# Fused look-ups in a product-key search: 128 narrow instructions a tile in place of 12 wide ones

## What is computed

```python
scores, idx = top_k(sim, 16)              # sim: (2, ..., 8 heads, 64 keys)
index = idx[0][:, None] + 64 * idx[1][None, :]      # 16 x 16 candidates
score = scores[0][:, None] + scores[1][None, :]
final_scores, pk_idx = top_k(score, 16)
final_indices = take_along_axis(index, pk_idx)      # the look-up
k = einsum(softmax(final_scores), keys_table[final_indices + head * 4096])
v = einsum(softmax(final_scores), values_table[...])
```

## Time and profile before

| | |
|---|---|
| median of 3 runs | 8583.4 us (8580.13 to 8584.05) |
| profiled execution, its own time | 8587.36 us |
| its span, first to last instruction | 8585.5 us |
| DVE busy | 4933.7 us, 57% of the span, 16123 instructions |
| PE busy | 6138.6 us, 71% |
| POOL busy | 5943.7 us, 69%, of which 6144 gathers |
| ACT busy | 3293.3 us, 38% |

### The profile page before, as it was taken

How to read it: one execution, slowest core, us unless ns; L and a number is a source line. 1 busy time by engine, 2 the same in 40 slices (tenths; PEclk the granted TensorE clock), 3 DMA queues, 4 the chain that set the end, 5 groups by cost and what they waited for, 6 DMA issues and landing times.

```text
span 8585.5 us, 111803 instructions
## 1 busy us (share of the span) xinstructions
PE 6138.6 (71%) x30064; PEld 4636.8 (54%) x30064; DVE 4933.7 (57%) x16123; ACT 3293.3 (38%) x9885; POOL 5943.7 (69%) x6159
## 2 busy tenths in 40 slices
PE   6869979787887879687887879787886875233222
PEld 5648656666565647666565656656465652122112
DVE  1246484947566574847566574857667473646522
ACT  1213334444443444434443444444443443333232
POOL 0007667777777777777777777777777777777775
PEclk7765666666766666566766666566766665555555
DMA  1102222222222222222222222222222222121111
GB/s 30 17 4 65 52 53 58 59 61 60 63 60 58 60 59 61 60 61 60 62 59 58 59 60 61 60 61 60 60 60 58 61 59 53 52 53 52 52 53 41
DMA packets 660626, 471.64 MB, mean 55 GB/s; under 512 B 560624, under 2 KB 561008, under 8 KB 659632
## 3 DMA queue, kind: packets, MB, share of 16 engines
q0 software_dynamic: 196608, 403.05, 17.8%
q1 hardware_dynamic: 463344, 60.87, 4.5%
HBM read 461.32 MB, written 2.10 MB: 54 GB/s over the span
## 4 chain that ended last, share of the span: by engine, by line
POOL 59%; issue 20%; PE 14%; DVE 4%; SPq 1%; DVEq 1%; ACT 1%; DMA 1%; POOLq 0%; ACTq 0%
POOL GATH L700 59%; PE MM L477 3%; PE MM L492 1%; DVE KV L923 1%; PE PB L1320 1%; PE PB L1308 1%; PE PB L1256 1%; PE PB L1287 1%; PE MM L429 1%; PE MM L513 1%; PE MM L516 1%; PE PB L1328 1%; PE MM L452 1%; PE TP L486 1%; SPq L371 0%
## 5 line engine op out<-in xcount | busy, mean ns | idle before, releaser
L700 POOL DMA_INDIRECT GATH<-in_table,IDX x6144 | 5937.5, 966 | 2590.9 <-issue 2505.0
L916 ACT ACTIVATE GATH<-GATH,WT 128x128 f32<-128x128 f32 x6144 | 1884.1, 390 | 1966.9 <-DMA GATH<-in_table,IDX 1966.1
L923 DVE TENSOR_REDUCE KV<-GATH 128x128 f32<-128x2048 f32 x384 | 1392.0, 3625 | 1165.3 <-ACT GATH L916 1157.7
L477 PE MATMUL MM<-SPEC,SW 128*128 128x8 f32 (+1 forms) x8800 | 1150.8, 288 | 103.0 <-DMA SW<-in_sw 68.9
L477 PEld LDWEIGHTS MM<-SPEC,SW 128*128 128x128 f32 (+1 forms) x8800 | 1143.0, 248 | 141.1 <-issue 138.3
L586 DVE COPY TURN<-TP 80x512 f32<-80x512 f32 (+1 forms) x512 | 345.1, 684 | 451.5 <-PE TP L509 275.0
L1423 PE MATMUL PB<-AREA 128*64 128x64 f32 (+1 forms) x2304 | 320.3, 300 | 392.1 <-ACT AREA L1198 391.9
L1423 PEld LDWEIGHTS PB<-AREA 128*64 128x64 f32 (+1 forms) x2304 | 257.7, 194 | 474.4 <-issue 426.0
L429 PE MATMUL MM<-F,TURN 128*128 128x80 f32 x2048 | 371.1, 341 | 197.4 <-DVE TURN L586 192.4
L429 PEld LDWEIGHTS MM<-F,TURN 128*128 128x128 f32 x2048 | 341.9, 252 | 249.4 <-issue 186.6
L545 ACT ACTIVATE U<-MM 128x320 f32<-128x320 f32 (+1 forms) x416 | 218.8, 526 | 636.7 <-PE MM L429 388.1
(11 more groups left out here) (223 smaller groups left out, 10065.5 us busy)
## 6 DMA issues: line engine op xcount, KB each, us to landing
GATH<-in_table,IDX POOLq DMA_INDIRECT x6144
SW<-in_sw SPq DMA_DIRECT2D x1280, 40.0 KB
CONV<-in_cwb SPq DMA_DIRECT2D x128, 4.0 KB
CONV<-in_cwb SPq DMA_DIRECT2D x128, 0.1 KB
U<-in_xT SPq DMA_DIRECT2D x16, 96.0 KB
out<-OUTB SPq DMA_DIRECT2D x16, 96.0 KB, 1.9
W1E<-in_w SPq DMA_DIRECT2D x1, 512.0 KB
W2E<-in_w SPq DMA_DIRECT2D x1, 512.0 KB
```

Source lines behind the costliest of these rows:

```text
L477: m = e.matmul(pv[r, :, k, :], SW[r, half, k % HM, w:w + WID * beside], Sv[r, :, c * MODES + k, :], start=True, stop=True)
L700: e.indirect_dma_start(GATH[:, r, k, :], None, table, bass.IndirectOffsetOnAxis(IDX[:, u // H, u % H, k:k + 1], 0)).then_inc(gath[r], 16)
L916: m = e.activation(GATH[:, r, k, :], GATH[:, r, k, :], ACT.Copy, scale=WT[:, u // H, u % H, k:k + 1])
L923: e.tensor_reduce(KV[:, u // H, :, u % H, :], GATH[:, u % RING, :, :].rearrange("p k (c d) -> p c d k", c=2), AX.X, ALU.add).then_inc(S["g ...
```

## The change

The two wide instructions of each group and the drain between them become one `scalar_tensor_tensor` for each head and result: (IOTA is_equal place) mult CI, where `place` is now a scalar for each partition, read through a pointer, and IOTA and CI are plain rows of 20 or 50. A group of four heads has 4 x 8 = 32 of them, 20 wide; a group of two heads has 16 of them, 50 wide. That is 2 x 32 + 4 x 16 = 128 instructions a tile for 12. The products land in the same places of EQ; the drain, the `tensor_reduce` and all the rest stay.

```diff
                     hit = EQ[:, 0:nh * 8 * nc].rearrange("p (h k c) -> p h k c", h=nh, k=8)
                     place = PF[:, h0:h0 + nh, k0:k0 + 8]
-                    e.tensor_tensor(hit, IOTA[:, 0:nc].rearrange("p (a b c) -> p a b c", a=1, b=1).to_broadcast([128, nh, 8, nc]),
-                                    place.rearrange("p h (k o) -> p h k o", o=1).to_broadcast([128, nh, 8, nc]), ALU.is_equal)
-                    e.drain()
-                    e.tensor_tensor(hit, hit, CI[:, h0:h0 + nh, 0:nc].rearrange("p h (o c) -> p h o c", o=1).to_broadcast([128, nh, 8, nc]), ALU.mult)
+                    for h in range(nh):
+                        for k in range(8):
+                            e.scalar_tensor_tensor(hit[:, h, k, :], IOTA[:, 0:nc], place[:, h, k:k + 1], CI[:, h0 + h, 0:nc], ALU.is_equal, ALU.mult)
                     yield TOP_STEPS * t + 6 + (g + 0.6) * 4 / len(LOOKUPS)
                     e.drain()
                     e.tensor_reduce(place, hit, AX.X, ALU.add); e.drain()
```

## The result

The changed kernel takes 8618.03 us (median of 7 runs, 8605.19 to 8639.52) against 8584.05 for the kernel before (7 runs, 8578.38 to 8587.86): ratio 1.0043, interval 1.0034 to 1.0053. The forecast was 20 us less; it is 34 us more. The time lies inside the stated range, but on the other side of the kernel before. The profiled execution of the changed kernel took 8623.13 us, its span is 8620.9. All medians and intervals here are of fast runs; one slow execution of a kernel of the experiments, 12140 us long, is left out.

What follows compares the result with a forecast made beforehand. It took POOL's gathers to bind from about 1500 us on. Relief of 85 us, new holds of 25 and a start cost of 40 summed to -20 us: 8563.5 us for the median, range 8520 to 8665.

Steps and rivals of the forecast that it cites:

- What bounds the kernel, two regimes, 85 us to be had on POOL: Until about 1500 us PE and DVE bind, then POOL's gathers; removing the wide operations saves POOL about 85 us.
- the 957 that the prediction named: Mean gather on POOL from 1500 to 8066 us, forecast near 957 ns in place of 967.
- Price on DVE: New instructions 141 and 172 ns from start to start, 50 ns of it a pointer; DVE 9 us a tile more.
- the rival without overlap: On DVE each new instruction waits for the one before, 225 to 256 ns; +94 us, 8677; chance 0.15.
- The rule that the prediction set against narrow operations: On DVE an operation costs (N+151)/0.96 ns, the next waits for an empty pipe; 24.8 us, sum about +5.
- New holds on POOL: Gathers beside the new narrow bursts lose 0.03 us a us over 42 tiles: 25 us, bounds 0 and 100.
- The start: Ahead of POOL's steady run, DVE's 9 us a tile count for 4.5 tiles: 40 us, not given back.
- After 1500 us: the 27 us more a pair have cover ... Cost there: nothing.: In the steady part DVE stays ahead of POOL, with 42.9 us a pair of waits for gathered rows; cost zero.
- 43 to 55 by the rivals: DVE's waits for gathers, us a pair, set against 60 us more a pair if the new instructions do not overlap.
- the third of the signs of being wrong: POOL begins to wait for L923, DVE's sums, in the steady part; the forecast had almost none after 1500 us.
- begins to suffer: Steady part suffers near 0.21 us an instruction on DVE; without overlap 5 to 17 us a pair uncovered; chance 0.15.

## Why the prediction was wrong, point by point

- *What bounds the kernel, two regimes, 85 us to be had on POOL*: right. The gathers lost 128 us to long ones before and 38 after, by adding up what each has over 947 ns; 90 less. The mean from 1500 to 8066 is 951 ns, even below the 957 that the prediction named.
- *Price on DVE*: nearly right. 150 and 181 ns from start to start for 141 and 172 predicted; 10.1 us a tile for 9, and DVE busy up by 507.5 us for about 430. By the prediction's prices for the rest, that puts a pointer scalar at about 60 ns and not 50, an estimate. Neighbours overlap, so the rival without overlap is out. The rule that the prediction set against narrow operations is only half of what the page says: in the Trainium skill ("VectorE: DVE Perf Modes", the section on the DRAIN) it goes on that a next operation that is not held starts earlier. The trace agrees with that: 150 and 181 ns from start to start for 232 and 264 of duration.
- *New holds on POOL*: 25 us predicted, under 10 found (beside the fused instructions of 50; beside those of 20 under 1). Too high. In sum the gathers have 38 us over 947 ns, no more than without any look-up.
- *The start*: 40 us predicted, 41.7 measured, and that so close a match is luck: the profiled execution of before began its search 9 us late. The runs with 3.4 us (+12) and 10.3 us (+43) more a tile give about 4 tiles' worth too, counted from that same execution.
- *"After 1500 us: the 27 us more a pair have cover ... Cost there: nothing."* This is the step that failed, and with it the sum. I took DVE's 42.9 us of waits for ACT's products in a pair (43 to 55 by the rivals) as cover. Over ten pairs they are 50.0 us a pair, of which 37 stay when POOL has half the work, since ACT itself then stands behind work for which PE is not ready; in the one shown above it is the experts' hidden layer. The real cover was 26 us by the periods (488 - 462), and between 20 and 31 by the runs with DVE time added. The change adds 30 us of DVE a pair, which lengthened the chain by 26, from 462 to 488. POOL's waits for L923 in the steady part, 106.6 us, are the third of the signs of being wrong that the prediction had named.
- And the same step had a second fault that no row can be blamed for: it measured the cover against POOL's old 488 us. The relief takes POOL to 482 to 484, so each us won on POOL is one less of cover. Gain on the bounding engine and cost on the one behind it do not add up; the period is, nearly, the larger of the two. With a chain of 488, the relief of 11 pairs was worth little: every second pair had it and the other lost it again, 489.2 us in the mean against 490.7 with the same DVE time and no relief. Only the last three, whose chain is shorter, kept theirs (-20 us).
- Of the rivals the one that "begins to suffer" named the right place, and a limit of 43 to 55 us a pair that was twice too high.

What stays open: why every second pair pays and the other does not, why the mean of both, 489.2, is a little above the chain alone (487.6), and why a gather that begins in a hold is held as often as it is.

## What to carry to other kernels

Before a wait is counted as cover, follow it one engine further: a wait for an in-order engine is slack only as far as that engine itself waits for the bounding one. A better reading is a run with the bounding engine's work halved; its period is close to the length of the next chain, and cover is the difference. Runs with some time added to the engine in question check it. Read waits over whole cycles of the loop, not over one pair: here 42.9 us in one window, 50.0 in the mean. And compare the lengthened chain with the bound as the change leaves it, not as it was: relief eats cover.

## What the runs showed of the hardware that I had not expected

- Beside the 3072 fused instructions with 20 elements POOL's gathers lose under 1 us in all, beside the 3072 with 50 under 10, while the 576 comparisons and products of 640 and 800 elements cost them some 90 us.
- The same 384 operations of 800 elements cost POOL's gathers 73 us in the kernel before, 90 with only the groups of 20 fused, 55 with 10.3 us a tile added, and a plan that only moves two sums changed the mean gather from 967 to 973 ns. A difference of 10 or 20 us in this kernel can be no more than that.
- The changed kernel scatters more: 8605 to 8640 us, against 8578 to 8588 for the one before. Why is not shown; with 3.4 us a tile added, where POOL still binds, ten runs lie between 8587 and 8611 as well.
